# Token attention: outputs loaded ahead of the next queries, norms moved rounds forward, outputs turned ahead of the queries' projection

## The reference

```python
x = x + L0_attn_a(layernorm(x))   # softmax attention, 16 heads
x = x + L0_ffn(layernorm(x))
x = x + L0_attn_b(layernorm(x))   # softmax attention, 4 wide heads
x = x + L0_ffn(layernorm(x))
x = x + L1_attn_a(layernorm(x))   # retention with decay
x = x + L1_ffn(layernorm(x))
x = x + L1_attn_b(layernorm(x))   # token attention, the layer that is changed
x = x + L1_ffn(layernorm(x))
```

```python
q = _split_qk(x @ Wq.T, b, n) * SCALE          # (b, n, 32, 8)
k = _split_qk(x @ Wk.T, b, n)
v = (x @ Wv.T).reshape(b, n, H, 2 * D).transpose(0, 2, 1, 3)
att = softmax(nan_to_num(einsum('bnqd,bnkd->bnqk', q, k)))   # 32 x 32 for each token
diff = att[:, :, :H, :H] - lam * att[:, :, H:, H:]
out = einsum('bnah,bhnd->bnad', diff, v)
out = out * rsqrt(mean(out * out, axis=-1, keepdims=True) + EPS) * (1.0 - LAM_INIT)
out = out.reshape(b, n, DIM) @ Wo.T + bo
```

## Time and profile before

| | us |
|---|---|
| median of 3 runs | 1280.55 (1278.72 to 1281.66) |
| profiled execution | 1274.09 |
| its span | 1272.3 |
| PE busy (mean granted clock 0.852) | 1039.2 (82%) |
| PEld busy | 920.5 (72%) |
| DVE busy | 700.2 (55%) |
| ACT busy | 389.3 (31%) |
| POOL busy | 321.1 (25%) |

### The profile page before, as it was taken

How to read it: one execution, slowest core, us unless ns; L and a number is a source line. 1 busy time by engine, 2 the same in 40 slices (tenths; PEclk the granted TensorE clock), 3 DMA queues, 4 the chain that set the end, 5 groups by cost and what they waited for, 6 DMA issues and landing times.

```text
span 1272.3 us, 21464 instructions
## 1 busy us (share of the span) xinstructions
PE 1039.2 (82%) x8114; PEld 920.5 (72%) x8114; DVE 700.2 (55%) x1410; ACT 389.3 (31%) x711; POOL 321.1 (25%) x356
## 2 busy tenths in 40 slices
PE   3589978757888885677878999998888887689998
PEld 3466655456777764655657999997788887689998
DVE  4468865435445436687875544435456655534443
ACT  1146544313343231233434323321121221222332
POOL 5300101025643573412111021100033333331000
PEclk9679997769999995798988999976667775599999
DMA  8735330000011000275430000335566665210000
GB/s 235 228 115 156 107 102 3 1 1 17 18 50 35 1 1 1 72 218 143 128 106 1 1 1 1 85 74 112 104 108 125 113 123 97 34 34 9 18 18 18
DMA packets 147431, 89.39 MB, mean 70 GB/s; under 512 B 109632, under 2 KB 136256, under 8 KB 146560
## 3 DMA queue, kind: packets, MB, share of 16 engines
q1 hardware_dynamic: 142960, 70.45, 23.3%
q10 hardware_dynamic: 2944, 12.59, 3.4%
q0 software_dynamic: 1424, 4.98, 1.2%
HBM read 54.16 MB, written 33.55 MB: 69 GB/s over the span
## 4 chain that ended last, share of the span: by engine, by line
PE 60%; DVE 23%; issue 6%; ACT 4%; POOL 3%; DMA 2%; SPq 2%; DVEq 0%; ACTq 0%; POOLq 0%
PE SC L386 21%; PE SC L2060 9%; PE pb L386 7%; PE OT L386 6%; PE pa L386 3%; DVE mx L1352 3%; PE OT L1924 2%; PE OT L2087 2%; PE SC L1879 2%; PE SC L1908 2%; PE pa L2259 2%; DVE V L1518 1%; DVE ON L1609 1%; PE OT L2358 1%; DVE r L1509 1%
## 5 line engine op out<-in xcount | busy, mean ns | idle before, releaser
L386 PE MATMUL SC<-xT_h,w_h 128*128 128x256 f32 x512 | 149.1, 291 | 8.1 <-DVE xT_l L1666 5.8
L386 PE MATMUL SC<-xT_l,w_h 128*128 128x256 f32 x512 | 147.0, 287 | 0.0
L386 PE MATMUL SC<-xT_h,w_l 128*128 128x256 f32 x512 | 146.4, 286 | 0.0
L386 PEld LDWEIGHTS SC<-xT_h,w_h 128*128 128x128 f32 x512 | 99.3, 194 | 11.5 <-DVE xT_l L1666 9.6
L386 PE MATMUL OT<-w,Qs 128*128 128x256 f32 x768 | 104.2, 285 | 2.2 <-DVE Qs L1676 1.4
L1352 DVE TENSOR_REDUCE mx<-SC 128x4 f32<-128x1024 f32 x64 | 78.1, 1220 | 41.8 <-PE SC L1879 41.4
L386 PEld LDWEIGHTS SC<-xT_h,w_l 128*128 128x128 f32 x512 | 99.3, 194 | 0.0
L386 PEld LDWEIGHTS SC<-xT_l,w_h 128*128 128x128 f32 x512 | 99.1, 194 | 0.0
L386 PEld LDWEIGHTS OT<-w,Qs 128*128 128x128 f32 x768 | 96.4, 191 | 2.9 <-DVE Qs L1676 1.6
L1672 DVE TENSOR_TENSOR hidden_f<-SC,silu_gate 128x512 f32<-128x512 f32 x64 | 44.0, 688 | 67.7 <-ACT silu_gate L1179 67.7
L777 POOL TENSOR_SCALAR ve<-mv 128x2 f32<-128x2 f32 x32 | 7.1, 222 | 292.9 <-DVE mv L1477 111.5
(11 more groups left out here) (414 smaller groups left out, 2855.6 us busy)
## 6 DMA issues: line engine op xcount, KB each, us to landing
Qs<-q_stack SPq DMA_DIRECT2D x56, 128.0 KB, 2.9
k_stack<-KT_h SPq DMA_DIRECT2D x16, 256.0 KB, 2.4
k_stack<-KT_l SPq DMA_DIRECT2D x16, 256.0 KB, 2.9
q_stack<-QT_h SPq DMA_DIRECT2D x16, 256.0 KB, 2.3
q_stack<-QT_l SPq DMA_DIRECT2D x16, 256.0 KB, 2.8
b_Q<-q_groups SPq DMA_DIRECT2D x64, 64.0 KB
o_groups<-b_O ACTq DMA_DIRECT2D x8, 512.0 KB, 3.0
Qs<-q_stack SPq DMA_DIRECT2D x56, 64.0 KB, 2.9
```

Source lines behind the costliest of these rows:

```text
L386: ins = pe.matmul(out_ap, left[a], right[b], start=first and n == 0, stop=last and n == len(terms) - 1, **more)
```

## The change

Offsets are changed and lines moved inside `at_slot`; no instruction is added, removed or altered. SP's `load_out` goes from 13 to 9 and to the head of its slot, ahead of `load_q`. On POOL `clipped` goes from 16 to 11 and `token_heads` from 17 to 13. ACT's `squares` goes from 17 to 12 and to the end of the slot, DVE's `square_sums` from 17 to 13. The turn of the outputs and both parts of its split go from 20 to 18, ahead of the queries' projection on PE, of `QT_h` on ACT and of `QT_l` on DVE.

```diff
--- before.py
+++ after.py
@@ -641,6 +641,8 @@
                                              o_groups[b % 2, o_row[i]:o_row[i] + 16].rearrange("a (g d) -> g a d", d=16)).then_inc(sig.sem["oload"], 16)
 
                         def at_slot(g):
+                            for b in due(g, 9):
+                                load_out(b)
                             for b in due(g, -7):
                                 load_q(b)
                             for b in due(g, 2):
@@ -649,8 +651,6 @@
                                 store(b, "ql", "qstore", "qload", 16 * 3 * GROUP, QT, q_groups)
                             for b in due(g, -12):
                                 store(b, "kl", "kstore", "kload", 32, KT, k_groups)
-                            for b in due(g, 13):
-                                load_out(b)
                             for b in due(g, -11):
                                 store_v(b)
                         return at_slot
@@ -844,9 +844,9 @@
                                 todo[b // 2]()
 
                 def tokens_at(g):
-                    for b in due(g, 16):
+                    for b in due(g, 11):
                         clipped(b)
-                    for b in due(g, 17):
+                    for b in due(g, 13):
                         token_heads(b)
                     for b in due(g, -13):
                         row_bias(b)
@@ -1116,8 +1116,6 @@
                             heads_out(b, h)
                     for b in due(g, 9):
                         store_out(b)
-                    for b in due(g, 17):
-                        squares(b)
                     for b in due(g, -7):
                         load_k(b)
                     for b in due(g, 1):
@@ -1126,6 +1124,8 @@
                         load_q(b)
                     for b in due(g, -16):
                         high(b, x_pair(s, b), pa, "xT", "vp", 1, "xh")
+                    for b in due(g, 18):
+                        high(b, aT, OT[1], "aT", "y", 1, "ah")
                     for b in due(g, -14):
                         high(b, QT, pb, "qp", "qstore", 64, "qh")
                     for b in due(g, -13):
@@ -1134,8 +1134,8 @@
                         probs(b, 1)
                     for b in due(g, -12):
                         v_out(b)
-                    for b in due(g, 20):
-                        high(b, aT, OT[1], "aT", "y", 1, "ah")
+                    for b in due(g, 12):
+                        squares(b)
                 return at_slot
 
             def ffn0(s):
@@ -1533,15 +1533,15 @@
                         residual(b)
                     for b in due(g, -16):
                         low(b, x_pair(s, b), pa, "xh", "xl")
-                    for b in due(g, 17):
-                        square_sums(b)
                     for h in range(TT):
                         for b in due(g, 1 + h):
                             less_maximum(b, h)
+                    for b in due(g, 18):
+                        low(b, aT, OT[1], "ah", "al")
                     for b in due(g, -14):
                         low(b, QT, pb, "qh", "ql")
-                    for b in due(g, 20):
-                        low(b, aT, OT[1], "ah", "al")
+                    for b in due(g, 13):
+                        square_sums(b)
                     for b in due(g, -13):
                         low(b, KT, pa, "kh", "kl")
                     for h in range(TT):
@@ -2114,14 +2114,14 @@
                     for h in range(TT):
                         for b in due(g, h):
                             scores(b, h)
+                    for b in due(g, 18):
+                        a_turned(b)
                     for b in due(g, -14):
                         q_out(b)
                     for b in due(g, -13):
                         k_out(b)
                     for b in due(g, -12):
                         v_out(b)
-                    for b in due(g, 20):
-                        a_turned(b)
                 return at_slot
 
             def ffn0(s, turn, tokens_out):
```

## The result

The changed kernel takes 1310.59 us in the median of 6 runs (1304.93 to 1314.14), the kernel before 1280.18 us (1278.72 to 1281.66): a ratio of 1.0259, 95% interval 1.0231 to 1.0287. It is 30.4 us slower; forecast were 1310.3 us and a range of 1302 to 1320. The profiled execution has a span of 1303.9 us where the kernel before had 1272.3.

The account below looks back on a forecast made before the run. Waits between engines were taken as the bound, `xn` of the item ahead standing on the path. Terms +36.0 +1.35 -0.3 -0.6 +0.3 +0.8 +0.6 -8.4 gave +29.75 us, added to the 1280.55 median: 1310.3 us, range 1302 to 1320.

Parts of the forecast that it names:

- heads ahead of `rstd`, four rounds, with the slower turn of `xn`: POOL's slot 5: `rstd` waits behind the heads, 9.0 us a round, +36.0; `xn` transposes at slow clock, +1.35 us.
- turn ahead of the projections (all up to the end of the weights), rounds 1 to 4: PE, ACT, DVE: projections 0.6 us later, `aT_l` fits DVE's idle; net -0.1 us in rounds 2 to 4, -0.3 in all.
- round 5: Last weights turned sooner on PE, scores at T+14.0, -0.6 us; outputs' load ahead of the queries' +0.3.
- round 6: SP: a late store could delay the queries' load, on whose landing this round's path runs; +0.8 us.
- round 7, sums ahead of `xT_l`: DVE: `ssq` of item 6 stands in front of the feed-forward stage's first `xT_l`, on the path; +0.6 us.
- tail, two items: Feed-forward start: earlier heads and turn end PE's waits; item 6 5.4 us less, 0.4 given back, item 7 3.4; -8.4 together.
- The load: SP's `load_out` ahead of the queries' load: +0.8 us in round 6, +0.3 in round 5; bounds 0 and 3 together.
- Clip: POOL's clip waits for load and previous item's turn, ready before DVE needs it; no cost beyond `ssq`'s counted 0.6 us.
- The tail without gain: Rival: ACT and DVE stop at item 7's squares and sums until its load lands; +38.1 us, 1318.7; chance 0.12.
- heads later than thought: Rival: clip, load or squares miss DVE's slot; 2 us late in four rounds gives +38, 1318 us; chance 0.08.
- the faster case: Rival: in POOL's slot 5 the heads don't hold up `xn`, rounds keep 34.1 us; -7.6 us, 1273; chance 0.04.

Follow-up runs that it names:

- the doubled power: The changed kernel with the power instruction of `token_heads` issued twice, the first into an overwritten place; profiled execution alone, span 1330.7 us.
- `row_bias` ahead of clip: The changed kernel with turn back at 20, sums and heads at 14 behind `rstd_of`, POOL's `row_bias` before `clipped`; 1272.05 us, ratio 0.9950 to the kernel before.

## Why the prediction was right

The steps, as the prediction put them, against the two traces:

| step | forecast | measured |
|---|---|---|
| heads ahead of `rstd`, four rounds, with the slower turn of `xn` | +37.35 | +37.0 |
| turn ahead of the projections (all up to the end of the weights), rounds 1 to 4 | -0.3 | +2.5 |
| round 5 | -0.3 | +0.1 |
| round 6 | +0.8 | +0.1 |
| round 7, sums ahead of `xT_l` | +0.6 | +0.6 |
| tail, two items | -8.4 | -8.5 |
| sum | +29.75 | +31.8 |

- *The heads.* From the end of the weights to the start of the scores it was 3.97, 3.65, 3.64 and 3.65 us before, and 12.92, 12.91, 12.90 and 13.19 after: 37.0 us. The choice of 8.24 us for the five instructions, the time with DVE idle, was right: 8.26 in rounds 1 to 3. No cover hid any of it, as the doubled power shows, and the loss was in the order of POOL's list. The 0.45 us a round for the slower turn of `xn` came, but not from the long idle alone: with the heads behind `rstd_of` the turn also took 1.12 us in rounds 2 to 4, and 0.66 with `row_bias` ahead of clip, where the turn of the outputs is late.
- *The turn.* Here a size was off: -0.3 us forecast, +2.5 measured, 0.3 of it in round 1, where nothing is turned yet. I had reckoned 0.6 us of delay for the projections, and took 0.69 off for `aT_l`. In the changed kernel `KT_l` is over at T+7.0 to T+7.2 in rounds 2 to 4, before at T+5.7 to T+5.8, 1.2 to 1.5 us later, and the weights by 0.6 to 0.9. In round 4 the mean granted clock in the 5.8 us behind T was 0.54, before 0.66 in 4.35 us: the clock rose to 2.4 GHz at T+5.0 to T+5.4 instead of T+3.1 to T+3.4 (by the first projection matmul of the short kind), and the projections ran longer at 1.2 GHz. With the heads behind `rstd_of` it rose at T+3.9, T+3.3 and T+3.1, the mean in round 4 was 0.71 over 5.2 us, `KT_l` came at T+6.1 to T+6.5, and the weights ended 0.1 us later to 0.2 us earlier than before, near the -0.1 a round of the forecast. So the price of the turn itself was right, and what had no place in the sum was the later rise of the clock. It does not come from the order ahead of the projections: with the power doubled and the same order there, the clock rose at T+3.1, T+2.7 and T+5.4. What sets it is open.
- *Round 5.* PE turned the last weights 0.65 us sooner after their end, as forecast (0.6), but the weights ended 0.8 us later by the same late clock.
- *The load.* Its bound was set at 0 to 3 us and it cost about nothing: PE's scores waited 1.2 us in all for `b_Q`, before 0.8. The reason was incomplete: I named the store as what `load_out` waits for, and not `hn`. In the changed kernel that is over in time, so the number came out, but the load alone loses 12.8 us in rounds 1 to 6.
- *Clip.* That it waits for the turn of the item before was put in, and that DVE could be held by what follows it on POOL was not; in the changed kernel the turn is early enough for this not to matter.
- *The tail.* 4.9 and 3.6 us, forecast 5.0 and 3.4. The back-reckoning of ACT's squares against the load was close enough: the first item took 25.0 us, and 24.9 had been forecast.
- *The rivals.* The tail without gain, heads later than thought, and the faster case all fell by the rounds above. The last of them became a kernel when the order of the two operations was turned: 1273 us by its sum, 1272.54 measured.
- *The median.* That 1310.3 met 1310.59 so closely is luck: the stretches sum to 31.8 us where 29.75 was forecast, and the six runs spread over 9 us. The profiled execution took 1305.71 us for a forecast 1303.8.

## What to carry to other kernels

Where an order is written out by hand in offsets of a period, reduce both to the period before an operation is moved: it comes in front of someone else's item, and that item may be on the path. A POOL chain of 8 us is free only while nothing short and urgent is queued behind it; write the short one first. And look up all waits of a moved operation, the one for its buffer too: it may be early moves of others that make its new place possible.

## What the runs showed of the hardware

- POOL's power over 128x32 elements took 5.46 us in the kernels before and after (5.43 to 5.63 in all runs) and over 128x2 0.71 to 0.73 in `rstd`, against 0.25 us for most multiplications of 128x32.
- DVE's L1513 took 0.24 us, and 1.03 to 1.34 where a 1.27 us POOL operation on 128x512 was running; both ended within 0.04 us of each other. The profile shows such a hold as a long instruction and not as a wait.
- Four issues of 64 KB on SP's queue took 2.7 to 3.8 us in the kernel before, and 6.5 to 7.3 us directly behind the queries' loads (8 on SP's queue, 4 on ACT's); they landed 2.5 to 3.8 us after their issue there, and the first three of each four 5.2 to 7.5 us after it here.
- Over the same order of work ahead of it, the clock rose to 2.4 GHz at T+5.0, T+5.2 and T+5.4 in rounds 2 to 4 of two executions of the changed kernel (0.54 over the first 5.8 us of round 4), and at T+3.9, T+3.3 and T+3.1 with the heads behind `rstd_of` (0.71 over 5.2 us).
